# A routed feed-forward stage: the second bias once per token instead of once per block, and three moves of order

## The chip, the core and the metric

The kernel runs on one core of a Trainium2 chip. The metric is device time in microseconds for one launch. The core has five engines with instruction streams of their own: TensorE (PE; PEld is its weight load), VectorE (DVE), ScalarE (ACT), GpSimd (POOL) and SyncE (SP). They meet through semaphores. SyncE and GpSimd also issue the DMAs, each on a queue of its own; 16 DMA engines serve both queues.

## What is computed

```python
def reference(x, src, dst, edge_type_8, ...):
    x = x + gnn(layernorm(x), src, dst, edge_type_8, ...)      # graph layer, 8 relations, gate
    x = x + ffn(layernorm(x)[None], Wr, br, W1, b1, W2, b2, gamma, beta)[0]
    return x

def ffn(tgt, Wr, br, W1, b1, W2, b2, gamma, beta):             # tgt: 1250 tokens x 1024
    logits = einsum('bsd,ed->bse', tgt, Wr) + br               # 8 experts
    top_v, top_i = top_k(logits, 2)
    router_w = sum(one_hot(top_i) * softmax(top_v)[..., None], axis=-2)
    h = relu(einsum('bsd,efd->bsef', tgt, W1) + b1)            # 512 hidden
    o = einsum('bsef,edf->bsed', h, W2) + b2                   # b2: one row of 1024 for each expert
    return layer_norm(tgt + einsum('bsed,bse->bsd', o, router_w)) * gamma + beta
```

The change lies in `ffn` alone. A token's output is its row plus, for each of its two experts, the share times (hidden times W2, plus that expert's b2).

## The kernel before

The tokens are ten tiles of 128 rows (the last has 98). After the graph layer and its gate (until 1718 us of the profiled execution) each tile is normalized, and its rows are stored three times: to the output, to `t_rows` (what the experts read) and to `sum_rows` (where the experts' parts are added). TensorE makes the router's logits from a high and a low half of each row; for this a tile gives two columns per expert, and `turn_logits` (L1312) turns them to rows and adds the halves with a small matmul pair. VectorE then picks the top two (L1449 on).

The routing stage (1718 to 1737 us) sorts the 2500 (token, expert) pairs into at most 27 blocks of 128 rows, so that a block has one expert. VectorE builds one-hot tables, TensorE multiplies them into a list of tokens (L1567) and a list of shares (L1573), and VectorE writes `token_at` and `row_at`, the addresses of a block's token rows and sum rows.

The expert stage (from 1737 us) goes through the blocks b = 0 to 26. All products take the operands apart into a high and a low part and make three matmuls for one. TensorE's order in block b (L2177 on) is: `first(b)`, 24 matmuls with W1; `token_tile(b + 1)`, 8 transposes of the next block's token rows; `second(b - 1, 0)`, the left half of the product with W2 of the block before; `hidden_transposed(b)`; `second(b - 1, 1)`, the right half. Each half of `second` begins with one matmul of 72 rows that puts the block's b2 into PSUM (L2136: a one-hot column `bias_at` against b2, of which the high and low parts lie at rows 0 and 32).

ScalarE splits the token rows (`token_hi`), makes the hidden layer and writes the block's output, times the share, to one of two slots of `o_s` (`output`, L1869). VectorE makes the low parts.

GpSimd's queue (L1820 on) has in block b: for b under 10, add beta to ten tiles of the output, one in each; `gather_tokens(b + 3)`, the rows of a block three further on; `scatter(b - 1)` (L1787), the add of a block's 128 output rows to `sum_rows`. A scatter waits until ScalarE has written both halves of the output and until the scatter before has landed. `output(b, 0)` waits until scatter b - 2 has landed, since it writes the same slot. SyncE's queue loads the experts' split weights, two halves of 4 MB for each expert, into a ring of four halves; a load waits until the half before has landed and until TensorE is done with the expert two before.

The end: when the first 22 scatters have landed, GpSimd loads all ten tiles of `sum_rows` (L1792) into `acc`, where ScalarE and VectorE normalize them beside the last blocks (`bulk_stats`, `scale`); the finished tiles are added to the output by indirect DMAs that leave out tokens with a row in the last five blocks (`store_bulk`, L1816). Tokens of the last five blocks (22 to 26) are done at the very end: `gather_sums` (L1796) fetches their sums into `acc` tiles 0 to 3 and one token slot, so the stores of tiles 0 to 3 have to land first; then come statistics and scaling, and `place` (L1808) adds them to the output.

## Time and profile before

| | |
|---|---|
| time, median of 3 runs | 2137.72 us (2135.85 to 2140.92) |
| the profiled execution | 2136.19 us, of which its span is 2134.5 us |
| busy: PE, DVE, ACT, POOL | 2010.5, 1252.6, 985.2, 921.5 us (94%, 59%, 46%, 43% of the span) |
| gate stage ends, routing ends, experts begin on PE | 1718, 1737, 1743 us |
| PE's last matmul ends | 2100 us |

A row of the timeline has the start in us from the span's start, the time the group took, the engine, the line, the operation with output and inputs, the count, and in brackets how long the engine stood idle before it and what ended that. A matmul's time runs until its result is out; the next one starts earlier, so what one costs is the distance between starts. A DMA row on POOL or SP is the issue; the transfer lands later.

### The profile page before, as it was taken

The page shows a single profiled execution, that of the slowest core. Times are in us where ns is not written, and L with a number is a line of the kernel's source. Part 1 is how long each engine was busy: PE and PEld are TensorE (multiplying, and loading weights), DVE is VectorE, ACT ScalarE, POOL GpSimd, SP SyncE. Part 2 cuts the span into 40 slices and gives each one's busy share as a digit, 9 for nine tenths or more (in the row PEclk, how much of TensorE's full clock was granted, in tenths as well). Part 3 has the DMA queues.
Part 4 walks back from the last instruction along what each step waited for, and adds up shares of the span by engine and source line. Part 5 has one row for each costly group of instructions (what it writes and reads, how often), then busy time and mean ns, then how long its engine had stood idle before and what let it go on. Part 6 is the DMA issues. An engine that isn't in the chain of part 4 may idle for free. (4 is left out here: it accounts for less than half of the span.)

```text
span 2134.5 us, 27951 instructions
## 1 busy us (share of the span) xinstructions
PE 2010.5 (94%) x9385; PEld 1599.8 (75%) x9385; DVE 1252.6 (59%) x2315; ACT 985.2 (46%) x1541; POOL 921.5 (43%) x813
## 2 busy tenths in 40 slices
PE   7999999999999999999989999899889859999993
PEld 6777777777777777787868777677478748788882
DVE  7589878852222222216999988888978842222245
ACT  3211122222222222217999999999844313333355
POOL 0000036555556656406777878778600012221226
PEclk9999999999999999999999999999999959999997
DMA  5322277787778777768788889989867579998757
GB/s 187 104 81 78 76 246 248 252 267 256 252 248 263 248 253 251 251 203 296 260 307 300 321 287 335 338 301 319 296 188 236 172 300 326 332 285 294 223 135 156
DMA packets 156360, 521.55 MB, mean 244 GB/s; under 512 B 31362, under 2 KB 31746, under 8 KB 154186
## 3 DMA queue, kind: packets, MB, share of 16 engines
q1 hardware_dynamic: 83706, 308.63, 41.5%
q0 software_dynamic: 72528, 211.35, 32.2%
q8 instruction: 67, 1.10, 0.2%
q14 instruction: 59, 0.48, 0.1%
HBM read 385.49 MB, written 156.25 MB: 254 GB/s over the span
## 5 line engine op out<-in xcount | busy, mean ns | idle before, releaser
L221 PE MATMUL psum<-w_hi,xnT_hi 128*128 128x512 f32 (+1 forms) x1592 | 420.2, 398 | 9.9 <-issue 5.0
L221 PE MATMUL psum<-w_lo,xnT_hi 128*128 128x512 f32 (+1 forms) x1592 | 419.5, 394 | 0.0
L221 PE MATMUL psum<-w_hi,xnT_lo 128*128 128x512 f32 (+1 forms) x1592 | 413.0, 394 | 0.0
L590 ACT ACTIVATE work<-psum 128x512 f32<-128x512 f32 (+1 forms) x150 | 89.6, 598 | 674.7 <-PE psum L221 674.7
L924 POOL DMA_INDIRECT sorted_rows<-acc x313 | 337.4, 1078 | 116.4 <-issue 84.8
L221 PEld LDWEIGHTS psum<-w_hi,xnT_hi 128*128 128x128 f32 (+1 forms) x1592 | 292.3, 186 | 80.5 <-issue 9.1
L221 PEld LDWEIGHTS psum<-w_lo,xnT_hi 128*128 128x128 f32 (+1 forms) x1592 | 295.4, 186 | 74.4
L221 PEld LDWEIGHTS psum<-w_hi,xnT_lo 128*128 128x128 f32 (+1 forms) x1592 | 294.6, 185 | 71.9
L1040 POOL DMA_INDIRECT w_hi<-y_rows,sort_row x168 | 226.7, 1350 | 63.8 <-issue 40.7
L1040 POOL DMA_INDIRECT w_lo<-y_rows,sort_row x164 | 215.8, 1316 | 62.7 <-issue 42.1
L1125 DVE SCALAR_TENSOR_TENSOR w_hi<-w_hi,sort_recip,y_hi 128x1024 fp32r<-128x1024 f32 x168 | 213.7, 1283 | 35.7 <-ACT y_hi L1086 30.7
L1165 PE MATMUL psum<-y_hi,hot 128*128 128x512 f32 x664 | 213.5, 403 | 12.9 <-ACT y_hi L1086 12.4
L1125 DVE SCALAR_TENSOR_TENSOR w_lo<-w_lo,sort_recip,y_hi 128x1024 fp32r<-128x1024 f32 x164 | 207.9, 1283 | 29.8 <-ACT y_hi L1086 25.5
L212 DVE TENSOR_TENSOR w_lo<-w_raw,w_hi 128x1024 fp32r<-128x1024 f32 x86 | 104.9, 1225 | 189.0 <-ACT w_hi L206 188.4
L892 DVE TENSOR_TENSOR acc<-acc 128x1024 fp32r<-128x1024 f32 x64 | 78.5, 1226 | 220.5 <-ACT acc L599 220.5
L1086 ACT ACTIVATE y_hi<-w_hi,sort_recip 128x1024 fp32r<-128x1024 f32 x168 | 192.1, 1144 | 12.9 <-DMA w_hi<-y_rows,sort_row 3.7
L1086 ACT ACTIVATE y_hi<-w_lo,sort_recip 128x1024 fp32r<-128x1024 f32 x164 | 187.6, 1144 | 10.4 <-DVE w_lo L1125 1.7
L1165 PEld LDWEIGHTS psum<-y_hi,hot 128*128 128x128 f32 x664 | 125.1, 192 | 51.2 <-ACT y_hi L1086 17.5
L921 POOL TENSOR_TENSOR gate_word<-gate_word 1x1 f32<-1x1 f32 x40 | 12.0, 300 | 345.0 <-DVE acc L860 204.6
L1787 POOL DMA_INDIRECT sum_rows<-o_s,row_at x25 | 39.6, 1585 | 241.2 <-DMA sum_rows<-o_s,row_at 130.2
L1051 ACT ACTIVATE apart<-lanes,sort_local 128x128 f16<-128x128 f32 x332 | 127.2, 386 | 6.0 <-DVE lanes L1100 6.0
L1172 PE MATMUL psum<-w_hi,hot 128*128 128x512 f32 x336 | 111.2, 413 | 7.5 <-DVE w_hi L1125 7.1
(378 smaller groups left out, 2645.0 us busy)
## 6 DMA issues: line engine op xcount, KB each, us to landing
split_experts<-acc SPq DMA_DIRECT2D x128, 512.0 KB
ring<-split_experts SPq DMA_DIRECT2D x16, 4096.0 KB, 15.7
w_raw<-in_wchunks SPq DMA_DIRECT2D x86, 512.0 KB, 5.1
y_rows<-work SPq DMA_DIRECT2D x144, 256.0 KB, 2.8
acc<-in_wchunks SPq DMA_DIRECT2D x64, 512.0 KB, 6.0
work<-local_rows SPq DMA_DIRECT2D x26, 384.0 KB, 4.5
acc<-in_bias SPq DMA_DIRECT2D x10, 512.0 KB, 5.6
sorted_rows<-acc POOLq DMA_INDIRECT x313, 4.6
```

The lines of the kernel that those rows point to most:

```text
L212: v.tensor_tensor(w_lo[:, s, q * PIECE:(q + 1) * PIECE], raw_piece(c, q), w_hi[:, s, q * PIECE:(q + 1) * PIECE].bitcast(F32), ALU.subtract)\
L221: i = pe.matmul(to[:rm, :], x_[:, k, m * P:m * P + rm], w_[:, s, k * HALF:(k + 1) * HALF], start=(n == 0), stop=(n == 3 * KD - 1))
L590: act.activation(stage_y[:rows(m), t % 4, :], bank[t % 4][:rows(m), :], ACT.Copy)\
L892: v.tensor_tensor(x_lo[:, p % 2, :], x_raw[:, p % 2, :], x_hi[:, p % 2, :].bitcast(F32), ALU.subtract).then_inc(x_lo_done, 1)
L924: pool.indirect_dma_start(sorted_dram, IndirectOffsetOnAxis(ap=e_dest[:, c:c + 1], axis=0), e_rec[:, c, :], None, bounds_check=BLOCKS * P ...
L1040: pool.indirect_dma_start(slot_of(b).bitcast(F32), None, y_dram, IndirectOffsetOnAxis(ap=sort_row[:, COLUMN[j]:COLUMN[j] + 1], axis=0), bo ...
L1051: act.activation(apart[:, k, :], lanes[:, :], ACT.Square, bias=sort_local[:, at:at + 1], scale=-1.0)\
L1086: act.activation(y_hi[:, j % 2, :], slot_of(b).bitcast(F32), ACT.Copy, scale=sort_recip[:, COLUMN[j]:COLUMN[j] + 1]).then_inc(hi_done, 1)
L1125: v.scalar_tensor_tensor(out=slot_of(b), in0=slot_of(b).bitcast(F32), scalar=sort_recip[:, COLUMN[j]:COLUMN[j] + 1], in1=y_hi[:, j % 2, :] ...
L1165: o = pe.matmul(bank[two + q], hot[:, h, k, :], y_hi[:, j % 2, q * HALF:(q + 1) * HALF], start=first, stop=False)
L1172: o = pe.matmul(bank[two + q], hot[:, h, k, :], slot_of(b)[:, q * HALF:(q + 1) * HALF], start=False, stop=last)
L1787: pool.indirect_dma_start(sum_dram, IndirectOffsetOnAxis(ap=row_at[:, b:b + 1], axis=0), o_s[:, b % 2, :], None, compute_op=ALU.add).then_ ...
```

## The change

1. **The second bias.** The bias matmuls of `second` go. Routing now makes a table `route_of` (for each token its shares of the eight experts, three times: twice the share and once what rounding takes from it). In blocks 2 to 11 TensorE turns one tile of the table (`turn_route`), ScalarE copies it, TensorE multiplies it with b2 (`biases`, two matmuls), and VectorE copies the result to `acc`. In blocks 12 to 21 GpSimd adds one tile of it to `sum_rows` (`add_bias`).
2. **Logits.** The small sum over the halves is taken for tiles 0 to 7 ahead of the last tile's transposes, and for tiles 8 and 9 together at the end.
3. **Routing.** VectorE writes `token_at` and `row_at` ahead of the last one-hot table; it also makes `route_of`.
4. **The end.** The sums of blocks 24, 25 and 26 are gathered into the three token slots, so two tiles of `acc` are needed again and not four. Tiles 0 and 1 are scaled ahead of a tile's statistics in block 25 and stored ahead of the last scatter; gamma is loaded by GpSimd in block 21.

```diff
-B2_AT = (0, 32)
+B2_AT = (0, 32, 64)
...
+                    if s == TILES:
+                        turn_logits(TILES - 2, range(TILES - 2))
...
-                        if m == TILES - 1:
-                            turn_logits(TILES - 1, range(TILES - 1))
...
-                turn_logits(TILES, [TILES - 1])
+                turn_logits(TILES, [TILES - 2, TILES - 1])
...
             def sum_slot(f):
 
-                return t_s[:, 0, :] if f == LAST else acc[:, f - FIRST_LATE, :]
+                if f < LAST - 2:
+                    return acc[:, f - FIRST_LATE, :]
+                return w_raw[:, 0, :] if f == LAST else t_s[:, f - LAST + 2, :]
...
+                def add_bias(m):
+
+                    pool.wait_ge(bias_out, m + 1)
+                    pool.dma_start(sum_dram[m * P:m * P + rows(m), :], acc[:rows(m), m, :], accum_op=ALU.add)\
+                        .then_inc(bias_added, 16)
...
+                    if b == LAST - 1:
+                        for m in range(2):
+                            store_bulk(m)
+                    m = b - TILES - FIRST_BIAS
+                    if 0 <= m < TILES:
+                        pool.wait_ge(o_added, 16 * (b - 1))
+                        add_bias(m)
+                        if m == TILES - 1:
+                            pool.dma_start(gamma_bc[:, :], gamma[0:1, :].to_broadcast([P, D])).then_inc(const_in, 16)
+                        pool.wait_ge(bias_added, 16 * (m + 1))
                     if 1 <= b < LAST:
                         scatter(b - 1)
-                    if b == LAST - 1:
-                        for m in range(4):
-                            store_bulk(m)
                 pool.wait_ge(o_added, 16 * (LAST - 1))
-                pool.wait_ge(bulk_stored[0], 64)
                 pool.wait_ge(t_free, BLOCKS_T)
-                for f in range(FIRST_LATE, BLOCKS_T):
+                for f in range(LAST - 2, BLOCKS_T):
                     gather_sums(f)
-                for m in range(4, TILES):
+                pool.wait_ge(bulk_stored[0], 32)
+                for f in range(FIRST_LATE, LAST - 2):
+                    gather_sums(f)
+                for m in range(2, TILES):
                     store_bulk(m)
...
                     if b == LAST - 1:
+                        for m in (0, 1):
+                            scale(m)
                         bulk_stats(2, 5)
                     if b + 1 < BLOCKS_T:
                         token_hi(b + 1)
+                    m = b - FIRST_BIAS
+                    if 0 <= m < TILES:
+                        act.wait_ge(turned_then_biased, 2 * m + 1)
+                        act.activation(routeT[:, m % 2, :], bank[6][:B2_K, 0:P], ACT.Copy).then_inc(route_copied, 1)
...
                     hidden_lo(b)
+                    m = b - FIRST_BIAS
+                    if 0 <= m < TILES:
+                        v.wait_ge(turned_then_biased, 2 * m + 2)
+                        v.tensor_copy(acc[:rows(m), m, :], psum[:rows(m), 6:8, :].rearrange("p b n -> p (b n)")).then_inc(bias_out, 1)
...
-                    pe.matmul(bank[q], bias_at[:B2_K, b:b + 1].to_broadcast([B2_K, P]), b2_s[:, q * HALF:(q + 1) * HALF],
-                              start=True, stop=False)
...
+                def biases(m):
+
+                    pe.wait_ge(route_copied, m + 1)
+                    if m == 0:
+                        pe.wait_ge(b2_ready, 2)
+                    for q in range(2):
+                        i = pe.matmul(bank[6 + q][:rows(m), :], routeT[:, m % 2, 0:rows(m)], b2_s[:, q * HALF:(q + 1) * HALF],
+                                      start=True, stop=True)
+                    i.then_inc(turned_then_biased, 1)
```

GpSimd's queue from block 21 to the bulk load, before; `e_ostored` counts landed scatters, `e_oread` ScalarE's output halves, `e_tfree` read token slots, `f_bin0` to `f_bin2` the bulk rows:

```order
L1493 DMA t_s<-t_rows,token_at 128x1024 [waits e_tfree]
L1787 DMA sum_rows<-o_s,row_at 1408x1024 [waits e_ostored,e_oread]
L1493 DMA w_raw<-t_rows,token_at 128x1024 [waits e_tfree]
L1792 DMA acc<-sum_rows 128x1024 [waits e_ostored]
L1792 DMA acc<-sum_rows 128x1024 x8
L1792 DMA acc<-sum_rows 98x1024
L1787 DMA sum_rows<-o_s,row_at 1408x1024 [waits e_oread,f_bin2,e_ostored,f_bin1,f_bin0]
```

The same queue now, from block 20 on; `e_bout` counts VectorE's copies of the bias product and `e_badd` landed bias adds:

```order
L1494 DMA w_raw<-t_rows,token_at 128x1024 [waits e_tfree]
L1808 DMA sum_rows<-acc 128x1024 [waits e_bout,e_ostored]
L1802 DMA sum_rows<-o_s,row_at 1408x1024 [waits e_ostored,e_oread,e_badd]
L1494 DMA t_s<-t_rows,token_at 128x1024 [waits e_tfree]
L1808 DMA sum_rows<-acc 98x1024 [waits e_bout,e_ostored]
L1862 DMA gamma_bc<-in_gamma 128x1024
L1802 DMA sum_rows<-o_s,row_at 1408x1024 [waits e_ostored,e_oread,e_badd]
L1494 DMA t_s<-t_rows,token_at 128x1024 [waits e_tfree]
L1802 DMA sum_rows<-o_s,row_at 1408x1024 [waits e_ostored,e_oread]
L1494 DMA w_raw<-t_rows,token_at 128x1024 [waits e_tfree]
L1813 DMA acc<-sum_rows 128x1024 [waits e_ostored]
```

A bias add stands between each gather of token rows and the scatter of blocks 12 to 21, and both waits are on landings.

TensorE at the end of the gate stage, both kernels in one piece (L1368 makes logits, L1317 is the small sum, L157 a transpose):

```order
+L1317 MATMUL psum<-pair_sum,lgT 128x8 x8
 L157 MATMUL psum<-ident,acc 128x98 x8
 L1368 MATMUL psum<-opT_hi,wr_pair 16x128 x8
 L1368 MATMUL psum<-opT_lo,wr_pair 16x128 x8
-L1317 MATMUL psum<-pair_sum,lgT 128x8 x9
 L1368 MATMUL psum<-opT_hi,wr_pair 16x98 x8
 L1368 MATMUL psum<-opT_lo,wr_pair 16x98 x8
+L1317 MATMUL psum<-pair_sum,lgT 128x8
 L1317 MATMUL psum<-pair_sum,lgT 98x8
 L1377 MATMUL psum<-w_raw,r_tri 128x160
```

Eight of the nine sums moved up ahead of the last tile's transposes, and one moved down behind its logits.

GpSimd's end, before (from the last two scatters on):

```order
L1787 DMA sum_rows<-o_s,row_at 1408x1024 [waits e_ostored,e_oread] x2
L1816 DMA out<-acc,bulk_at 1250x1024 [waits f_scaled,f_x1b]
L1816 DMA out<-acc,bulk_at 1250x1024 [waits f_scaled] x3
L1796 DMA acc<-sum_rows,row_at 128x1024 [waits e_tfree,f_bst0,e_ostored]
L1796 DMA acc<-sum_rows,row_at 128x1024 x3
L1796 DMA t_s<-sum_rows,row_at 128x1024
L1816 DMA out<-acc,bulk_at 1250x1024 [waits f_scaled] x6
L1808 DMA out<-acc,final_at 1250x1024 [waits f_y,f_late]
```

And now, from the last scatter but one (`f_bst0` counts the first landed stores):

```order
L1802 DMA sum_rows<-o_s,row_at 1408x1024 [waits e_ostored,e_oread]
L1837 DMA out<-acc,bulk_at 1250x1024 [waits f_scaled,f_x1b]
L1837 DMA out<-acc,bulk_at 1250x1024 [waits f_scaled]
L1802 DMA sum_rows<-o_s,row_at 1408x1024 [waits e_ostored,e_oread]
L1817 DMA t_s<-sum_rows,row_at 128x1024 [waits e_tfree,e_ostored]
L1817 DMA t_s<-sum_rows,row_at 128x1024
L1817 DMA w_raw<-sum_rows,row_at 128x1024
L1817 DMA acc<-sum_rows,row_at 128x1024 [waits f_bst0]
L1817 DMA acc<-sum_rows,row_at 128x1024
L1837 DMA out<-acc,bulk_at 1250x1024 [waits f_scaled] x8
L1829 DMA out<-acc,final_at 1250x1024 [waits f_y,f_late]
```

Two stores moved ahead of the last scatter, two behind the gathers, and three gathers no longer wait for a store.

## Rows read from the trace of the kernel before

**Rows 1.** Busy us by stretch: PE, PEld, DVE, ACT, POOL; clock, DMA share, GB/s

```profile
1770.50:1901.40 130.90, 127.58 (x621) 105.97 (x620) 26.71 (x40) 41.20 (x100) 34.48 (x28) 1.00 0.97 309
1901.40:2003.10 101.70, 101.70 (x497) 84.90 (x496) 21.38 (x32) 33.20 (x80) 20.90 (x16) 1.00 0.88 300
```

**Rows 2.** Timeline of PE, one block of the expert stage

```profile
1901.43 3.79 PE L2126 MATMUL psum<-ring,tT_hi 128*128 x16
...
1906.88 1.04 PE L157 MATMUL psum<-ident,t_s 128*128 128x128 f32 x8
1907.67 0.48 PE L2136 MATMUL psum<-b_s,bias_at 72*128 72x512 f32 x1
1907.99 2.00 PE L2148 MATMUL psum<-ring,hT_hi 128*128 x8
...
1914.14 3.79 PE L2126 MATMUL psum<-ring,tT_hi 128*128 x16
```

**Rows 3.** The bias matmuls: count, ns min/median/max, first and last start, form

```profile
L2136 PE MATMUL psum<-b_s,bias_at x54: 399/481/792, 1764.1 to 2096.6; 72*128 72x512 f32 x54
```

**Rows 4.** Timeline of POOL: scatters (L1787) and the start of the bulk load

```profile
1896.54 1.57 POOL L1787 DMA_INDIRECT sum_rows<-o_s,row_at  x1 [14.67 <-DMA sum_rows<-o_s,row_at]
...
1911.94 1.57 POOL L1787 DMA_INDIRECT sum_rows<-o_s,row_at  x1 [12.49 <-ACT o_s L1869]
...
1919.57 1.57 POOL L1787 DMA_INDIRECT sum_rows<-o_s,row_at  x1 [4.71 <-issue]
...
1949.59 1.57 POOL L1787 DMA_INDIRECT sum_rows<-o_s,row_at  x1 [13.17 <-DMA sum_rows<-o_s,row_at]
...
1956.64 1.57 POOL L1787 DMA_INDIRECT sum_rows<-o_s,row_at  x1 [4.14 <-DMA sum_rows<-o_s,row_at]
...
2043.40 1.57 POOL L1787 DMA_INDIRECT sum_rows<-o_s,row_at  x1 [9.79 <-ACT o_s L1869]
...
2049.78 5.39 POOL L1792 DMA_DIRECT2D acc<-sum_rows  x10 [3.46 <-DMA sum_rows<-o_s,row_at]
...
2083.22 1.56 POOL L1787 DMA_INDIRECT sum_rows<-o_s,row_at  x1 [5.75 <-ACT acc L1919]
```

**Rows 5.** Line L1787, the 25 scatters: from issue to landing

```profile
DMA to landing us min/median/max: 6.1/11.3/17.0
```

**Rows 6.** Line L1301, the ten adds of the gate bias: from issue to landing

```profile
DMA to landing us min/median/max: 4.7/5.2/7.7
```

**Rows 7.** Timeline of SP's queue: weight loads (L1502), issues

```profile
1895.82 0.33 SPq L1502 DMA_DIRECT2D ring<-split_experts  x1
...
1914.49 76.60 SPq L1502 DMA_DIRECT2D ring<-split_experts  x5
```

**Rows 8.** Waits, 1764 to 2134 us: who for whom, total us, times, longest

```profile
POOL sum_rows L1787 <- DMA sum_rows<-o_s,row_at: 130.2, 14, 14.7
...
PE psum L157 <- DMA t_s<-t_rows,token_at: 3.5, 3, 3.0
```

**Rows 9.** Timeline of PE: end of the gate stage, start of the expert stage

```profile
1702.81 1.57 PE L157 MATMUL psum<-ident,acc 98*128 98x98 f32 x8 [5.97 <-DVE acc L1428]
...
1706.44 4.00 PE L1317 MATMUL psum<-pair_sum,lgT 16*128 16x8 f32 x18 [0.36 <-ACT lgT L1280]
...
1742.74 1.97 PE L157 MATMUL psum<-ident,t_s 128*128 128x128 f32 x8 [7.46 <-DMA t_s<-t_rows,token_at]
```

**Rows 10.** Timeline of ACT: first statistics of bulk rows and of late sums

```profile
2058.72 1.03 ACT L1897 ACTIVATE psum<-acc 128x1024 f32<-128x1024 f32 x1 [2.79 <-DMA acc<-sum_rows]
...
2107.45 1.06 ACT L1897 ACTIVATE t_s<-acc 128x1024 f32<-128x1024 f32 x1 [10.17 <-issue]
```

**Rows 11.** Timeline of POOL at the end: first gather of sums, two stores

```profile
2101.00 1.00 POOL L1796 DMA_INDIRECT acc<-sum_rows,row_at  x1 [7.50 <-issue]
...
2107.33 1.60 POOL L1816 DMA_INDIRECT out<-acc,bulk_at  x1 [0.30 <-issue]
2109.24 1.57 POOL L1816 DMA_INDIRECT out<-acc,bulk_at  x1 [0.31 <-issue]
```

More of the change, by code:

```diff
@@ L1316, in turn_logits @@
                     for m in tiles:
-                        i = pe.matmul(bank[2 if m < TILES - 1 else 3][:rows(m), m * E:(m + 1) * E], lgT[:, m * P:m * P + rows(m)], pair_sum[:, :],
+                        i = pe.matmul(bank[2 if m < TILES - 2 else 3][:rows(m), m * E:(m + 1) * E], lgT[:, m * P:m * P + rows(m)], pair_sum[:, :],
                                       start=True, stop=True)
@@ L1440, in _ @@
                 three_d, lg = [P, TILES, E], router[:, :, :]
-                for at, need, rm in ((slice(0, TILES - 1), 1, P), (slice(TILES - 1, TILES), 2, rows(TILES - 1))):
+                for at, need, rm in ((slice(0, TILES - 2), 1, P), (slice(TILES - 2, TILES - 1), 2, P),
+                                     (slice(TILES - 1, TILES), 2, rows(TILES - 1))):
                     v.wait_ge(lg_rows, need)
@@ L1623, in _ @@
                                         part_w[:, h, :].bitcast(F32).unsqueeze(2).to_broadcast([P, COLS, LISTS]), ALU.mult)
+                for k in range(2):
+                    i = v.tensor_tensor(shares[:, k, :, :], chosen[:, :, k * TILES:(k + 1) * TILES].rearrange("p e t -> p t e"),
+                                        weight_of[:, k, :].unsqueeze(2).to_broadcast([P, TILES, E]), ALU.mult)
+                link(i)
+                v.wait_ge(lists_done, 1)
+                v.tensor_scalar(empty[:, :], bank[2][:, 0:TILES_T], 0.0, None, ALU.is_equal)
+                link(v.tensor_scalar(tokens[:, :], bank[2][:, 0:TILES_T], -1.0, None, ALU.add))
+                v.scalar_tensor_tensor(out=token_at[:, :], in0=empty[:, :], scalar=float(Y_PAD), in1=tokens[:, :],
+                                       op0=ALU.mult, op1=ALU.add).then_inc(tabled, 1)
+                v.scalar_tensor_tensor(out=row_at[:, :], in0=empty[:, :], scalar=spare_row[:, 0:1], in1=tokens[:, :],
+                                       op0=ALU.mult, op1=ALU.add)
+                v.memset(route_of, 0.0)
+                link(v.tensor_tensor(shares[:, 0, :, :], shares[:, 0, :, :], shares[:, 1, :, :], ALU.add))
+                v.tensor_copy(route_of[:, :, B2_AT[0]:B2_AT[0] + E], shares[:, 0, :, :])
+                link(v.tensor_copy(shares_hi[:, :, :], shares[:, 0, :, :]))
+                v.tensor_copy(route_of[:, :, B2_AT[1]:B2_AT[1] + E], shares[:, 0, :, :])
+                v.tensor_tensor(route_of[:, :, B2_AT[2]:B2_AT[2] + E], shares[:, 0, :, :], shares_hi[:, :, :].bitcast(F32), ALU.subtract)
                 v.tensor_tensor(not_last[:, 0, :], place[:, 0:TILES], place[:, TILES:COLS], ALU.is_lt)
@@ L1846, in _ @@
                     place(f)
[L1847 removed]
+                pool.wait_ge(bulk_stored[1], 16 * (TILES - 2 + LATE))
             @block.scalar
@@ L1950, in _ @@
                         output(b - 1, 1)
-                    if b == LAST - 1:
-                        for m in (0, 1):
-                            scale(m)
-                for m in range(4, 8):
+                for m in range(4, 7):
                     scale(m)
-                act.wait_ge(t_free, BLOCKS_T)
-                for n, f in ((5, LAST - 4), (6, LAST - 3), (7, LAST - 2)):
+                late_stats(5, LAST - 2)
+                for m in range(7, 10):
+                    scale(m)
+                for n, f in ((6, LAST - 4), (7, LAST - 3)):
                     late_stats(n, f)
-                for m in (8, 9):
-                    scale(m)
                 for f in range(FIRST_LATE, LAST):
@@ L2147, in second, with turn_route @@
                             n += 1
-                            i = pe.matmul(bank[q], x_[:, k, :], w_, start=False, stop=(n == 3 * KF))
+                            i = pe.matmul(bank[q], x_[:, k, :], w_, start=(n == 1), stop=(n == 3 * KF))
                     i.then_inc(s2_done if q else o_first, 1)
+                def turn_route(m):
+                    if m == 0:
+                        pe.wait_ge(late_ready, 3)
+                    else:
+                        pe.wait_ge(bias_out, m)
+                    transpose(pe, bank[6][:B2_K, 0:P], route_of[:, m, :]).then_inc(turned_then_biased, 1)
+                def biases(m):
+                    pe.wait_ge(route_copied, m + 1)
+                    if m == 0:
+                        pe.wait_ge(b2_ready, 2)
[3 more added lines that the diff above has]
+                    i.then_inc(turned_then_biased, 1)
                 def spread_tokens():
```

62 lines of the change are left out of this document (29 added, 33 removed).

## The prediction

> **What bounds the kernel now.** I read the stretches by engine first [rows 1], then one block of the expert stage on TensorE [rows 2], then the chain of waits on GpSimd's queue [rows 4] and the list of waits [rows 8]. In blocks 12 to 19 TensorE is busy for all of 101.70 us and the 16 DMA engines for 0.88 of it [rows 1]. A block takes 1914.14 - 1901.43 = 12.71 us [rows 2], so TensorE is the bound. A second resource stands right beside it. GpSimd issues one scatter-add of a finished block to the sum rows at a time, and each waits until the one before has landed: 14 such waits, 130.2 us [rows 8]. I call the time from one such issue to the next, where only the landing decides, a step. It is 7.63 and 7.05 us where no weight load is under way, on average 7.3 (1911.94 to 1919.57 and 1949.59 to 1956.64 [rows 4]), and 15.4 us where a 4 MB load shares the engines (1896.54 to 1911.94, a load issued at 1895.82 [rows 4, 7]), so one load costs the chain 8.1 us. Five steps with three loads in them (1895.82, 1914.49 and the next some 19 us on [rows 7]) should then take 5 x 7.3 + 3 x 8.1 = 60.8 us; it was 1956.64 - 1896.54 = 60.1 [rows 4]. The chain needs about 12 us per block and has 12.71: it is nearly full. It already reaches TensorE, since the gather of token rows three blocks ahead stands behind each scatter on the same queue; TensorE stood 3.5 us for such rows [rows 8], in the stretch in which beta is also added to the output over that queue and the DMA share is 0.97 [rows 1].
>
> **The change part by part.** All sums are made against the profiled execution: span 2134.5 us, 2136.19 with the 1.7 us around it, 1.5 below the median of 2137.72.
>
> Logits. 4.00 us of small matmuls (the sum of two halves for nine tiles) lie between the logits of tile 8 and those of tile 9, while TensorE sat idle for 5.97 us just before, waiting for the last tile [rows 9]. The change puts eight of the nine tiles into that idle time; their inputs are there, since the last of them is tile 7. Two matmuls of tile 8 come back at the end (a half of 0.5 us) and one more small VectorE addition of 0.2. Nothing else ends that wait: **-3.3 us**.
>
> Token addresses. VectorE writes them ahead of a few small operations, about 1 us sooner, but also does some 2 us more for the new table of shares, and the second small sum is later. The first token rows land at 1742.74, after 7.46 us of waiting for a transfer that runs beside two weight loads [rows 9]; the added VectorE work ends ahead of that. I take 0, with 1 us to either side.
>
> TensorE in the expert stage. Each of the 54 bias matmuls [rows 3] holds the next matmul up by 1907.99 - 1907.67 = 0.32 us [rows 2], so 0.64 per block goes. In blocks 2 to 11 one transpose (about 0.15, from 8 in 0.79 [rows 2]) and two matmuls of the same 72-row form (0.64) come back: +0.15 per block. So by block 12 the work stands at -3.3 - 0.6 + 1.5 = -2.4 us. From block 12 on a block could take 12.07 us. ScalarE's copy of the shares and VectorE's copy of the bias product are hidden: a block leaves ScalarE two thirds and VectorE four fifths of its time [rows 1], and the next transpose that waits for VectorE's copy stands behind 5.4 us of first-layer matmuls. If that cover were gone, it would cost about 1 us in each of ten blocks.
>
> **GpSimd's queue, blocks 12 to 21.** Here the change adds a wait, and it decides. Ahead of each scatter now stands a bias add of 128 rows of 4 KB to the same sum rows: it waits until the last scatter has landed, and the next scatter waits until it has landed. Behind that stand, on the same queue, the scatter and then the token gather for a block two and a half blocks away, for which TensorE waits. No row shows such an add without other traffic. The nearest are the scatter, of the same size and into the same rows, at 6.1 us to landing at least [rows 5], and the add of the gate bias, same form and size but into SBUF, at 4.7, 5.2 at the median [rows 6]. A step is 1.2 us longer than the landing (7.3 against 6.1), so a bias add is a step of 5.9 to 7.3; I take 6.9, near the scatter. A pair takes 7.3 + 6.9 = 14.2 us, over 12.07 even without a load. The loads of the second half are issued from 1914.49 on over 76.60 us, five of them [rows 7], and wait for TensorE's progress, so they stay inside the chain however long it gets: four whole ones and some 0.6 of another. Ten pairs take 142 + 4.6 x 8.1 = 179 us. They begin when scatter 10 has landed, 1919.57 - 2.4 = 1917 [rows 4], so scatter 21 goes out at 2096 instead of 2043.40. Its slack is soon used up: a gather goes out two and a half blocks of 12.07 us ahead of its use and needs some 10 to land, so TensorE can run some 20 us (an estimate) ahead of the queue, and the first two or three pairs take that.
>
> End. The bulk load of the sum rows begins 6.4 us after scatter 21 (2043.40 to 2049.78 [rows 4]): 2102.4. From there to the last scatter it is 2083.22 - 2049.78 = 33.4 us now. It gets longer: ScalarE's program has two tile statistics, which wait 8.9 us for the first group (2049.78 to 2058.72 [rows 4, 10]), ahead of the token copy for block 25. TensorE now stands already and can do nothing in that time, and two scalings are also moved ahead of the copy for block 26. I take 38, between 33 and 42. After the last scatter it is 51.3 us now: 17.8 to the first gather of sums, of which 7.50 wait for four stores of bulk rows [rows 11], and 33.5 from there on. With three of the sums in free slots the first gather needs only the scatter's landing, 7.3; against that, eight stores instead of six lie ahead of the placements (2109.24 - 2107.33 = 1.9 each [rows 11]). ScalarE's statistics, which start 6.4 us after the first gather [rows 10, 11], run beside them, so of these 3.8 us I add 1.2: 7.3 + 33.5 + 1.2 = 42 us, so -9.3.
>
> **Sum:** 2102.4 + 38 + 42 = 2182.4 us of span, and 1.7 around it: 2184 us, 48 above the profiled execution.
>
> The Trainium skill's page "DMA: Bandwidth & Descriptors" (section "Anatomy of one DMA — SWDGE (gpsimd) path") speaks for a much cheaper add: about 2.0 us plus the bytes at 436 GB/s, an estimate of 3.2 us for 512 KB. The scatter of the same bytes took at least 6.1 [rows 5], so the trace does not agree; by that figure the pair would fit and the first rival would hold.
>
> **The rivals.** (1) *The add is short and hides; faster.* A block has 12.07 us, the scatter takes 7.3 and the loads 3.7 of it; with 20 us of lead to spend over ten blocks, a step of the add under about 3.1 us would leave TensorE the bound. Then -2.4, -6.4 for blocks 12 to 21, -3.2 for the five after, -9.3 at the end and +4.6 before the last scatter: 2136.2 - 16.7 = 2119.5 us. For it speaks that the DMA engines are idle for 0.12 of the time [rows 1]; against it that the shortest landing of a like add is 4.7 us, before any load [rows 6]. (2) *The engines' total time and not the waits is the limit.* The stretch with beta keeps them busy 0.97 x 130.90 / 10 = 12.7 us per block, the one without 0.88 x 101.70 / 8 = 11.2 [rows 1]. With bias adds in place of beta's, blocks 12 to 21 then stay at about 12.7 us as now, and the rest holds: 2136.2 - 2.4 - 3.2 - 9.3 + 4.6 = 2126 us. Against it: the waits stand in the program one behind the other. (3) *A load hits the add and the scatter alike.* Each 4 MB load then costs 16.2 instead of 8.1: +37, 2221 us. Against it: the load has a fixed number of pieces to put between the others, and the five-step check held with 8.1. (4) *Cheap adds, loads that fall into the waits between transfers:* steps of 6.4, half the price of a load: 137 + 18 = 155, so 2160 us.
>
> **How the numbers follow.** The main case has 0.68 (2165 to 2203), case 4 0.12, case 3 0.09, case 1 0.07, case 2 0.04. The range of 8 in 10 takes in the main case, most of case 4 and the lower part of case 3: 2150 to 2210. Faster by over 0.2% (about what a measurement tells from no change here): case 1 and most of case 2, 0.10. Within it, where cases 2 and 4 meet: 0.03. Slower: 0.87.
>
> **What would show it.** Right: in the waits of the expert stage, GpSimd's scatter and the new add each wait for the other's landing some ten times, a pair 14 us apart without a load and over 20 with one; TensorE stands for token rows in blocks 14 to 22, over 40 us together; the first gather of sums comes 7 to 8 us after the last scatter; the top two begin 3.3 us sooner. Wrong: pairs 12 us apart and TensorE busy throughout blocks 12 to 21 (case 1 or 2); pairs of 20 us and more after the last load (a step of the add far over 7).

## The result, and the profile after

| | before | after |
|---|---|---|
| time, median of 4 runs each | 2139.32 us (2135.85 to 2144.04) | 2177.17 us (2174.82 to 2181.03) |
| ratio, 95% interval | 1 | 1.0165 (1.0142 to 1.0188) |
| span of the profiled execution | 2134.5 us | 2178.9 us |

The change makes the kernel slower by 37.9 us. What runs ahead of the changed code takes some us more or less from run to run: the matmul that counts the chosen pairs (L1377) begins between 1708 and 1723 us in the profiles of this study. So I compare traces from that matmul on. From there to the end it is 417.8 us before (2134.5 - 1716.68) and 460.2 after (2178.9 - 1718.68): +42.4; ahead of it 3.6 are gained.

GpSimd's queue after; L1808 is the new bias add, L1802 the scatter, L1813 the bulk load, L1817 the late sums. Columns as in [rows 4].

```profile
1920.32 0.98 POOL L1808 DMA_DIRECT2D sum_rows<-acc  x1 [3.81 <-DMA sum_rows<-o_s,row_at]
1935.91 1.60 POOL L1802 DMA_INDIRECT sum_rows<-o_s,row_at  x1 [14.62 <-DMA sum_rows<-acc]
...
1953.44 0.95 POOL L1808 DMA_DIRECT2D sum_rows<-acc  x1 [14.54 <-DMA sum_rows<-o_s,row_at]
1959.18 1.60 POOL L1802 DMA_INDIRECT sum_rows<-o_s,row_at  x1 [4.80 <-DMA sum_rows<-acc]
...
2050.79 1.60 POOL L1802 DMA_INDIRECT sum_rows<-o_s,row_at  x1 [4.69 <-DMA sum_rows<-acc]
...
2057.24 0.95 POOL L1808 DMA_DIRECT2D sum_rows<-acc  x1 [3.48 <-DMA sum_rows<-o_s,row_at]
2063.01 1.60 POOL L1802 DMA_INDIRECT sum_rows<-o_s,row_at  x1 [4.82 <-DMA sum_rows<-acc]
...
2094.64 1.57 POOL L1802 DMA_INDIRECT sum_rows<-o_s,row_at  x1 [4.03 <-ACT o_s L1899]
...
2101.15 5.38 POOL L1813 DMA_DIRECT2D acc<-sum_rows  x10 [3.23 <-DMA sum_rows<-o_s,row_at]
...
2135.92 1.53 POOL L1802 DMA_INDIRECT sum_rows<-o_s,row_at  x1 [4.28 <-ACT o_s L1899]
2142.46 1.78 POOL L1817 DMA_INDIRECT t_s<-sum_rows,row_at  x1 [5.01 <-DMA sum_rows<-o_s,row_at]
```

Every add waits for a scatter and every scatter for an add. A pair takes 2063.01 - 2050.79 = 12.2 us where no weight load is under way. A step beside a load takes 15.6 (1920.32 to 1935.91) or 17.5 (1935.91 to 1953.44). The ten pairs take 2094.64 - 1920.32 = 174.3 us. TensorE leaves them 10 x 12.25 = 122.5.

Landing of the add (L1808) and of the scatter (L1802), after:

```profile
DMA to landing us min/median/max: 5.1/5.4/15.9
...
DMA to landing us min/median/max: 6.0/6.5/18.0
```

Waits from 1755 to 2180 us, after (total, times, longest), to be held against [rows 8]:

```profile
ACT o_s L1899 <- DMA sum_rows<-o_s,row_at: 129.1, 14, 25.2
...
POOL sum_rows L1802 <- DMA sum_rows<-acc: 77.2, 10, 15.2
POOL sum_rows L1808 <- DMA sum_rows<-o_s,row_at: 56.9, 10, 14.5
...
PE psum L157 <- DMA t_s<-t_rows,token_at: 33.5, 5, 16.3
```

The wait for each other is there in both directions, ten times each. It reaches ScalarE, which may not overwrite `o_s` (129.1 us; the row of before stands below), and TensorE, whose token rows stand behind it on the queue: 33.5 us where it was 3.5 [rows 8].

```profile
ACT o_s L1869 <- DMA sum_rows<-o_s,row_at: 4.6, 2, 2.4
```

TensorE after, four block starts and the three long stalls:

```profile
1772.29 3.79 PE L2163 MATMUL psum<-ring,tT_hi 128*128 x16
...
1785.14 3.79 PE L2163 MATMUL psum<-ring,tT_hi 128*128 x16
...
1963.75 3.79 PE L2163 MATMUL psum<-ring,tT_hi 128*128 x16
...
1976.00 3.79 PE L2163 MATMUL psum<-ring,tT_hi 128*128 x16
```

```profile
1954.35 1.97 PE L157 MATMUL psum<-ident,t_s 128*128 128x128 f32 x8 [5.30 <-DMA t_s<-t_rows,token_at]
...
1997.86 1.97 PE L157 MATMUL psum<-ident,t_s 128*128 128x128 f32 x8 [16.25 <-DMA t_s<-t_rows,token_at]
...
2046.11 1.97 PE L157 MATMUL psum<-ident,t_s 128*128 128x128 f32 x8 [8.34 <-DMA t_s<-t_rows,token_at]
```

A block with a bias tile takes 1785.14 - 1772.29 = 12.85 us (12.84 in most others), one without any bias 1976.00 - 1963.75 = 12.25; before it was 12.71 [rows 2]. Behind each long stall eight transposes take 1.97 us and not 1.04 [rows 2]: TensorE begins again at the lower of its two clock levels (1.2 GHz and not 2.4). The stretch around the first of them, columns as in [rows 1], has a granted clock of 0.55:

```profile
1953.00:1960.00 7.00, 5.56 (x18) 4.47 (x19) 2.58 (x4) 4.10 (x10) 1.77 (x2) 0.55 0.49 78
```

### The profile page after: what moved, and what is told of

Its sections match the earlier page's. It is cut to its first block and busy times, and to the rows that moved or that the text cites. A ratio compares the mean times of both kernels' runs of the same rounds, so it can differ in the third digit from the quotient of the medians.

```text
span 2178.9 us, 27955 instructions
## 1 busy us (share of the span) xinstructions
PE 2021.9 (93%) x9361; PEld 1605.8 (74%) x9361; DVE 1265.6 (58%) x2333; ACT 987.8 (45%) x1551; POOL 934.6 (43%) x824
## 5 line engine op out<-in xcount | busy, mean ns | idle before, releaser
L1086 ACT ACTIVATE y_hi<-w_hi,sort_recip 128x1024 fp32r<-128x1024 f32 x168 | 192.0, 1143 | 15.4 <-DMA w_hi<-y_rows,sort_row 5.4
L2015 DVE TENSOR_TENSOR hT_lo<-w_raw,hT_hi 128x512 fp32r<-128x512 f32 x26 | 18.0, 693 | 202.2 <-ACT hT_hi L1915 202.1
L1802 POOL DMA_INDIRECT sum_rows<-o_s,row_at x25 | 40.3, 1612 | 219.0 <-ACT o_s L1899 90.5
## 6 DMA issues: line engine op xcount, KB each, us to landing
ring<-split_experts SPq DMA_DIRECT2D x16, 4096.0 KB, 15.9
```

Of the source, the lines that this page charges most:

```text
L1086: act.activation(y_hi[:, j % 2, :], slot_of(b).bitcast(F32), ACT.Copy, scale=sort_recip[:, COLUMN[j]:COLUMN[j] + 1]).then_inc(hi_done, 1)
```

## The experiments

Theory A: the time goes into two accumulating DMAs that wait for each other on one queue, and a weight load lengthens each wait that it falls on. Rival B: the added traffic costs it. Rival C: the bias work of blocks 2 to 11 or the new order at the end costs it. The table gives each run's time beside the kernel before on the same chip, and the stretch from the counting matmul to the end of its profile (417.8 before, 460.2 after). A stretch belongs to one execution: that of x_add_16rows was the fastest of nine (2138.02 us), that of x_add_out the slowest of ten (2143.30), that of x_moves_fine 6.9 us over its median (2149.75). In x_logits the code behind the counting matmul is that of the kernel before, and the stretch is 4.2 us longer, so a difference of that size tells nothing.

| run | time | before there | ratio, 95% | stretch |
|---|---|---|---|---|
| x_no_add | 2133.31 | 2142.29 | 0.9939 (0.9914 to 0.9963) | 411.7 |
| x_add_out | 2136.65 | 2142.29 | 0.9977 (0.9963 to 0.9990) | 418.0 |
| x_moves | 2132.10 | 2142.29 | 0.9948 (0.9932 to 0.9965) | 414.3 |
| x_bulk_add | 2150.27 | 2142.29 | 1.0038 (1.0018 to 1.0059) | 435.3 |
| x_small_loads | 2132.71 | 2142.84 | 0.9954 (0.9939 to 0.9969) | 411.2 |
| x_add_pairs | 2161.90 | 2142.84 | 1.0092 (1.0076 to 1.0108) | 446.3 |
| x_add_16rows | 2148.02 | 2142.84 | 1.0028 (1.0011 to 1.0044) | 428.0 |
| x_logits | 2137.40 | 2142.84 | 0.9972 (0.9957 to 0.9986) | 422.0 |
| x_fine_loads | 2166.00 | 2142.41 | 1.0105 (1.0060 to 1.0150) | 442.4 |
| x_moves_fine | 2142.90 | 2142.41 | 0.9998 (0.9981 to 1.0016) | 428.2 |
| x_beta_late | 2136.94 | 2142.41 | 0.9963 (0.9945 to 0.9981) | 416.8 |
| x_moves_mixed | 2127.48 | 2144.33 | 0.9924 (0.9906 to 0.9941) | 407.3 |

**Without the adds.** In `for b`, `add_bias(m)` and its two waits go.

```diff
-                        pool.wait_ge(o_added, 16 * (b - 1))
-                        add_bias(m)
...
-                        pool.wait_ge(bias_added, 16 * (m + 1))
```

> The changed kernel without the ten adds of the bias tiles to the sum rows in blocks 12 to 21 and without their waits; the tiles are still made in blocks 2 to 11, so the second bias is missing from the output. Theory A (the two accumulations that wait for each other on GpSimd's queue cost the time): TensorE is the bound again in blocks 12 to 21, at 12.2 us per block, and the time is the kernel before less what the other parts give: 2139.3 - 3.6 (logits) - 6.4 (bias matmuls, 27 x 0.46 less 10 x 0.6) - 8.3 (end) + 1.4 (bulk load to last scatter) = 2122 us, between 2117 and 2128. Rival B (the 10 x 512 KB of added traffic cost it): also about 2122, since the traffic goes too. Rival C (the loss lies in the bias work of blocks 2 to 11 or in the new order at the end): 2155 or more.

C falls: the loss is gone with the adds. But 9 us are gained and not 17. Three of the nine single runs took 2122.5 to 2123.9 us, as A has it, the other six 2129.0 to 2138.3; the profile is of one of the six (2129.02). In the profile 411.7 us stand where 417.8 - 6.4 - 8.3 + 1.4 = 404.5 were expected. TensorE waits for token rows around block 9, where beta shares the queue:

```profile
1858.82 3.79 PE L2160 MATMUL psum<-ring,tT_hi 128*128 x16
1867.70 1.97 PE L157 MATMUL psum<-ident,t_s 128*128 128x128 f32 x8 [3.27 <-DMA t_s<-t_rows,token_at]
1877.85 3.79 PE L2160 MATMUL psum<-ring,tT_hi 128*128 x16
```

This block takes 1877.85 - 1858.82 = 19.03 us and not 12.84. Before, a block at the same place waits almost as long, 3.05 us (first row below), and takes 15.98. Nearly all of the difference is the clock: 0.71 here from the transposes on (last row), 1.00 before (second row).

```profile
1868.67 1.09 PE L157 MATMUL psum<-ident,t_s 128*128 128x128 f32 x8 [3.05 <-DMA t_s<-t_rows,token_at]
...
1868.00:1876.00 8.00, 7.33 (x38) 6.22 (x39) 1.29 (x2) 2.81 (x7) 3.70 (x3) 1.00 0.84 152
```

```profile
1867.00:1878.00 11.00, 10.30 (x40) 8.68 (x41) 1.29 (x2) 3.07 (x8) 3.69 (x3) 0.71 0.87 153
```

So 2.9 of the missing 7.2 us come from this block, 0.2 of them from a longer wait and the others from a lower clock behind it. Of the rest 1.5 lie at the end (2126.9 - 2082.39 = 44.5 us from the last scatter on, where 43.0 were counted on) and 1.2 in a block that waits for ScalarE's output (13.45 us and not 12.25, from 2001.52); I have not placed what is left.

**The same adds, but meeting no scatter.** The target of the ten adds is the output, and both waits go. In their place the first add waits until the adds of beta to the output have landed, and the bulk load until all ten bias adds have.

```diff
-                    pool.dma_start(sum_dram[m * P:m * P + rows(m), :], acc[:rows(m), m, :], accum_op=ALU.add)\
+                    pool.dma_start(out[m * P:m * P + rows(m), :], acc[:rows(m), m, :], accum_op=ALU.add)\
```

> The changed kernel with the ten adds of 512 KB from the same place of the queue, in the same form, but into the rows of the output and not of the sum rows: they meet no scatter, so neither waits for the other (one wait for all ten ahead of the bulk load). The second bias so reaches the output past the normalization. The traffic is that of the changed kernel. Theory A (waits): 2122 us as without the adds, and up to 10 more since an add stands ahead of a scatter on the same queue: 2122 to 2133; GpSimd's scatter and bias add no longer wait for each other, TensorE waits under 10 us for token rows. Rival B (traffic): nearly as slow as the changed kernel, 2160 or more.

B falls: with the full traffic the time is 3.3 us above the run without the adds, and 40 below the changed kernel. A has the mechanism; its range ended at 2133, 3.7 us short. The waits (total, times, longest) no longer name the add:

```profile
POOL sum_rows L1802 <- ACT o_s L1900: 145.1, 14, 15.0
...
POOL sum_rows L1802 <- DMA sum_rows<-o_s,row_at: 77.4, 9, 14.2
...
PE psum L157 <- DMA t_s<-t_rows,token_at: 9.8, 3, 4.8
```

**The other moves alone**, built from both kernels: bias by matmul as before, all else as after.

> The kernel before with the other moves alone (logits, order of the routing, three late sums in the token slots, two tiles scaled and stored sooner, gamma by GpSimd in block 21); the second bias by one matmul for each half in each block, as before. Theory A: 2139.3 - 3.6 (logits) - 8.3 (end) + 1.4 = 2129 us, between 2125 and 2133. Rival: if the end's gain came only from the sums being late anyway in the changed kernel, the end stays at 51 us and the time at 2136.

A holds. The end's gain is real: the last scatter goes out at 2088.07 and the span ends at 2131.2, so 43.1 us against 51.3 before. And the median is that of the run without adds (2132.1 and 2133.3): moving the bias off the matmuls would bring nothing at the median even if the adds were free. In three of nine runs it brought some 9 us (2122.5 to 2123.9); what decides between these runs and the others is not shown.

**The price of the loads.** From the twelfth half on a load fetches 64 of its 8192 columns.

```diff
+                        if n < SMALL_FROM:
+                            load_half(sp, n, row + n % 2 * P)
+                        else:
+                            sp.dma_start(ring[:, n // 2 % 2, n % 2, 0, 0:64].bitcast(F32),
+                                         we_dram[bass.ds(row + n % 2 * P, P), 0:64]).then_inc(half_in[n % RING], 16)
```

> The changed kernel with the last five weight loads (those issued beside the chain of bias adds and scatters) cut from 32 KB to 256 B per row, so that the last experts work with old weights; all adds and waits stay. In the changed kernel's trace a step of the chain is about 6 us without a load and 16 with one, five of twenty steps with one. Theory A (a load costs the chain 10 us each time, and the add itself some 6): ten pairs take 10 x 12.3 = 123 us and not 174, just TensorE's own 12.25 per block, and the time falls to that of the kernel without the adds, 2133 us, or up to 8 above: 2127 to 2141. Rival (the added wait itself is too long, loads or not): the time stays above 2157, less than 20 us gained.

A holds, and to the number. All waits and adds are there, and the chain keeps pace with TensorE: ten of TensorE's blocks without idle time (columns as in [rows 1]), then GpSimd's queue, first add, one pair and scatter 21.

```profile
1914.60:2037.00 122.40, 122.40 (x601) 102.30 (x600) 26.85 (x40) 41.25 (x100) 35.29 (x30) 1.00 0.65 116
```

```profile
1919.88 0.98 POOL L1813 DMA_DIRECT2D sum_rows<-acc  x1 [4.30 <-DMA sum_rows<-o_s,row_at]
...
1975.76 1.61 POOL L1807 DMA_INDIRECT sum_rows<-o_s,row_at  x1 [4.64 <-DMA sum_rows<-acc]
...
1987.88 1.59 POOL L1807 DMA_INDIRECT sum_rows<-o_s,row_at  x1 [4.67 <-DMA sum_rows<-acc]
...
2044.61 1.57 POOL L1807 DMA_INDIRECT sum_rows<-o_s,row_at  x1 [3.91 <-DMA sum_rows<-o_s,row_at]
```

Ten pairs in 2044.61 - 1919.88 = 124.7 us. In the changed kernel 174.3, with five loads: (174.3 - 124.7) / 5 = 9.9 us a load. So the mutual wait alone fits: a pair of 12.1 us here (1975.76 to 1987.88) against a block of 12.25. It is the loads that carry the chain past TensorE.

**The price of the bytes.** Sixteen rows and not 128 in each add, all waits kept.

```diff
-                    pool.dma_start(sum_dram[m * P:m * P + rows(m), :], acc[:rows(m), m, :], accum_op=ALU.add)\
+                    pool.dma_start(sum_dram[m * P:m * P + 16, :], acc[:16, m, :], accum_op=ALU.add)\
```

> The changed kernel with each bias add cut from 128 rows to 16, one row for each DMA engine; all waits stay, and the other rows lack the second bias. It tells the fixed price of the wait from that of the bytes. Theory A (most of an add's 5.4 us to landing is bytes and pieces of the load between them): step of the add under 4 us without a load and under 8 with one, chain under TensorE's 12.25 per block, 2131 to 2142. Rival (most is a fixed price of issue and landing): step over 5 us, and 2155 or more.

Both miss the time (2148.02, from 2138.02 to 2152.92; the profile is of the fastest run). The add's landing (first row) and four rows of GpSimd's queue:

```profile
DMA to landing us min/median/max: 2.7/2.7/12.2
```

```profile
1909.46 0.89 POOL L1808 DMA_DIRECT2D sum_rows<-acc  x1 [3.55 <-DMA sum_rows<-o_s,row_at]
1922.09 1.61 POOL L1802 DMA_INDIRECT sum_rows<-o_s,row_at  x1 [11.73 <-DMA sum_rows<-acc]
...
2020.70 0.88 POOL L1808 DMA_DIRECT2D sum_rows<-acc  x1 [3.35 <-DMA sum_rows<-o_s,row_at]
2023.68 1.62 POOL L1802 DMA_INDIRECT sum_rows<-o_s,row_at  x1 [2.11 <-DMA sum_rows<-acc]
```

Without a load the step is 3.0 us, as A says: of 5.4 us to landing 2.7 stay with 64 KB, and 2.7 are the other 448 KB. What A had wrong is the load. It holds up a 64 KB add too, in a step of 12.6 us the first time, and else it falls mostly on the scatter that comes next. The ten pairs take 2049.71 - 1909.46 = 140.3 us; without loads they would take 10 x 9.4 (6.4 for the scatter, 3.0 for the add), so a load still costs some 9 us (an estimate) beside adds of an eighth of the size.

**Two adds in one wait.** `add_bias(m - 1)` and `add_bias(m)` in every second block, and one wait for both.

> The changed kernel with the bias adds issued two at a time in every second block (rows of different tiles do not meet), with one wait for both: five waits of scatters for adds and not ten. Theory A (what is paid is the wait for a landing, not the bytes): two adds in flight land in 1 to 3 us more than one, so two blocks of the chain take 2 x 6.4 + 7 to 9 + one load's 10 = 30 to 32 us and not 34.9, 15 to 25 us in all: 2152 to 2162. Rival (an add costs by its bytes, one after the other): no gain, 2170 to 2180.

A holds, at its upper edge: 15.3 us less than the changed kernel. Two adds in flight make a step of 9.2 us without a load:

```profile
1970.90 1.88 POOL L1808 DMA_DIRECT2D sum_rows<-acc  x2 [3.26 <-DMA sum_rows<-o_s,row_at]
1980.13 1.60 POOL L1802 DMA_INDIRECT sum_rows<-o_s,row_at  x1 [7.35 <-DMA sum_rows<-acc]
```

**Bias rows kept off the chain.** Tiles are written plainly to memory of their own, the bulk load adds into the tiles that still hold the bias, and late sums are added onto gathered bias rows.

```diff
-                    pool.dma_start(sum_dram[m * P:m * P + rows(m), :], acc[:rows(m), m, :], accum_op=ALU.add)\
+                    pool.dma_start(bias_dram[m * P:m * P + rows(m), :], acc[:rows(m), m, :])\
...
-                    pool.dma_start(bulk_slot(m), sum_dram[m * P:m * P + rows(m), :]).then_inc(...)
+                    pool.dma_start(bulk_slot(m), sum_dram[m * P:m * P + rows(m), :], accum_op=ALU.add).then_inc(...)
```

> The changed kernel with the bias rows kept off the scatters' chain: in blocks 12 to 21 each tile is written plainly to rows of its own in memory, with no wait; the bulk load of the sum rows adds into the tiles in SBUF, which still hold the bias; the late sums are added onto bias rows that are gathered ahead of the last scatter's landing. Theory A: no wait between a scatter and the bias, so 2122 us as without the adds, and 0 to 6 more for ten plain writes, an adding bulk load and five small gathers: 2122 to 2128, under the moves alone by 1 to 7. Rival B (traffic): ten writes of 512 KB and ten adding loads cost 10 us or more: 2132 or above.

Theory A failed, mostly at the end of the kernel and not on the chain:

```profile
2050.60 9.09 POOL L1814 DMA_DIRECT2D acc<-sum_rows  x10 [3.42 <-DMA sum_rows<-o_s,row_at]
2080.50 2.13 POOL L1803 DMA_INDIRECT sum_rows<-o_s,row_at  x1 [20.82 <-DMA acc<-sum_rows]
...
2094.93 1.53 POOL L1803 DMA_INDIRECT sum_rows<-o_s,row_at  x1 [1.13 <-DMA sum_rows<-o_s,row_at]
```

From the bulk load to the next scatter 29.9 us pass, and 2066.29 - 2047.63 = 18.7 with plain loads in the run without adds:

```profile
2047.63 5.37 POOL L1813 DMA_DIRECT2D acc<-sum_rows  x10 [3.49 <-DMA sum_rows<-o_s,row_at]
2066.29 1.68 POOL L1802 DMA_INDIRECT sum_rows<-o_s,row_at  x1 [13.29 <-DMA acc<-sum_rows]
```

From the last scatter to the end it is 2148.1 - 2094.93 = 53.2 us, against 44.5 in the run without adds. One block also waits 3.65 us for token rows and takes 19.16. So rival B has the time (2132 or above). The adding loads still cost less than the waits that they save, since the time is 27 us below that of the changed kernel; they cost more than the whole change gains without the adds, and the version is 8 us slower than the kernel before.

**The logits alone.** The diff is that of the change.

> The kernel before with the move of the logits' small sums alone. Theory A: the top two begin 3.3 to 3.6 us sooner and all that follows moves with them: ratio 0.9984, 2139 of 2142. Rival: around block 10, while beta is added over the same queue, TensorE waits for token rows anyway, so what is gained ahead is lost there: ratio 1.000 within 0.001.

By the times the rival is out: the ratio's interval ends at 0.9986. Its centre, -6 us, is more than the move can give (3.6 in the trace); the interval reaches down to 3. The one profile does not bear this out: there TensorE stands 1.90 and 3.09 us for token rows in blocks 8 and 9 (0.27 and 3.05 before), and the stretch behind the counting matmul is 4.2 us longer. So what is gained ahead can be lost there, as the rival says, and in this execution it was.

**Shorter pieces.** Each row of a load is 32 KB in one piece; here eight DMAs of 4 KB a row, in the changed kernel and in the moves alone.

```diff
+            for j in range(LOAD_PIECES):
+                at = slice(j * (2 * CW // LOAD_PIECES), (j + 1) * (2 * CW // LOAD_PIECES))
+                sp.dma_start(ring[:, n // 2 % 2, n % 2, :, :].rearrange("p k n -> p (k n)")[:, at].bitcast(F32),
+                             we_dram[bass.ds(row, P), at]).then_inc(half_in[n % RING], 16)
```

> The changed kernel, all of it, but each 4 MB weight load is issued as eight DMAs of 512 KB whose pieces are 4 KB long and not 32 KB. Theory A: a load costs a step of the chain 10 us because its long pieces stand between the short ones (4 KB) of the add or scatter; with pieces of one size the engines are shared evenly, a step beside a load takes 2 to 4 us more and not 10, ten pairs 140 to 150 us and not 174, and the time is 2133 to 2145. Rival (a load costs by its bytes, which are the same): 2172 to 2182.

> The kernel before with the other moves (bias by matmul) and the same loads in 4 KB pieces. Theory A: the 5 to 7 us in which TensorE waits for token rows around blocks 8 to 10, beside loads and beta, shrink too: 2124 to 2131. Rival (the engines' total time is the limit in that stretch, 0.97 busy): 2132 as the moves alone, or a few us above since eight DMAs have more to begin and end.

All four forecasts miss the times (2166.00 and 2142.90). What A says of the stalls is half right. Blocks 2 to 11 run without a stall in both, at 12.84 and 12.71 us, and in the changed kernel the ten pairs take 2075.11 - 1913.51 = 161.6 us: less than 174.3, not the 140 to 150 of A. But loads follow one another, and in pieces each takes longer beside short DMAs: the halves beside beta are issued 23 to 27 us apart in the moves (from 1783.55 to 1884.52), and 18 to 20 in the kernel before. From block 12 on TensorE waits for weights (L1782 is where SyncE reports a landed half). The moves with 4 KB pieces (total, times, longest):

```profile
PE psum L2138 <- SPq L1782: 15.3, 3, 12.5
```

**Beta later**, in blocks 12 to 21: `if 12 <= b < 12 + TILES` in place of `if b < TILES`.

> The kernel before with the other moves, and beta added in blocks 12 to 21 and not in 0 to 9. In blocks 0 to 11 the DMA engines are 0.97 busy, in 12 to 21 0.75, and TensorE waits 5 to 7 us for token rows around blocks 8 to 10. Theory A (beta's adds cause that wait, and behind block 12 there is room for them since nothing waits for them): 2126 to 2129. Rival (there they lengthen the scatters' steps, the chain reaches TensorE as the bias adds did): 2132 or more.

The rival holds. TensorE waits no more in blocks 8 to 10, and instead in three blocks from 14 on, by 0.63, 3.30 and 2.10 us.

**Pieces mixed**: 4 KB for the seven loads beside beta, 32 KB for the others, on the moves alone.

```diff
+            return 8 if RING <= n < 11 else 1
```

> The kernel before with the other moves, and 4 KB pieces for the seven weight loads that run beside beta (the fifth to the eleventh half) alone; the first four and the last five keep 32 KB pieces. With 4 KB pieces throughout, TensorE no longer waited for token rows in blocks 8 to 10, but from block 12 on it waited 15 us for the weights, whose loads follow one another and take longer each. Theory A: with the pieces mixed, the first gain stays and the loss goes: the moves alone less 5 to 7 us, 2125 to 2129 at the level of the kernel before of 2142. Rival (the weight loads so delayed reach TensorE in the next blocks all the same, or the wait for token rows comes later): 2132 or more.

A holds, and this version is faster than both kernels: 16.9 us under the kernel before. Over the moves alone it gains 4.6 us (2132.10 to 2127.48): on the same chip its six runs all lie below the four of the moves, though the intervals of the two ratios overlap. TensorE has no idle time left in either stretch (columns as in [rows 1]):

```profile
1770.00:1900.00 130.00, 130.00 (x634) 108.38 (x633) 26.73 (x40) 42.37 (x105) 34.51 (x28) 1.00 0.95 277
1900.00:2060.00 160.00, 160.00 (x781) 133.41 (x781) 33.45 (x50) 54.19 (x130) 38.15 (x35) 1.00 0.84 274
```

## Why the prediction was right, step by step

The forecast was 2184 us, the time is 2177.17. That the add and the scatter wait for each other, that loads fall into these waits and that TensorE then stands for token rows is what the runs without waits and with small loads show. One step of the mechanism does not hold: a pair was to take 14.2 us, over TensorE's block "even without a load". It takes 12.2, and with small loads it hides; the loss shows only with the loads. That the total is so near is in part luck, as told below. In the trace it forecast +48 and +38.8 came (42.4 less 3.6). The terms:

| step | forecast | measured |
|---|---|---|
| last tile's transposes to counts | -3.3 | -3.6 (13.87 to 10.27) |
| counts to the first token tile | 0 | -0.4 (26.06 to 25.69) |
| bias matmuls, each block | 0.64 | 0.46 (12.71 to 12.25) |
| tile's transpose and two matmuls, net | +0.15 | +0.13 (12.84) |
| pair without a load | 14.2 us | 12.2 |
| a load | 8.1 us, 4.6 of them | 9.9, five of them |
| ten pairs | 179 us | 174.3 |
| bulk load to last scatter | 38 | 34.8 |
| last scatter to end | 42 | 43.0 |

**Logits and addresses** were right. TensorE from the last sums to the counts, after:

```profile
1702.79 1.95 PE L1317 MATMUL psum<-pair_sum,lgT 16*128 16x8 f32 x16 [0.35 <-ACT lgT L1280]
1708.41 1.57 PE L157 MATMUL psum<-ident,acc 98*128 98x98 f32 x8 [3.66 <-DVE acc L1428]
...
1713.93 0.56 PE L1317 MATMUL psum<-pair_sum,lgT 16*128 16x8 f32 x4 [0.33 <-ACT lgT L1280]
1718.68 0.87 PE L1377 MATMUL psum<-w_raw,r_tri 128*128 128x160 f32 x2 [4.19 <-DVE w_raw L1461]
```

Sixteen small matmuls take 1.95 us out of what was idle time (3.66 remain of 5.97 [rows 9]), and four stand at the end.

**TensorE's blocks.** The distance of 0.32 us behind a bias matmul overstated its price, since the next matmul's own wait is in it. Both prices came out lower, so the net of blocks 2 to 11 stayed. What the prediction left out is that work saved ahead of block 10 need not arrive behind it: TensorE waits around blocks 8 to 10 for token rows that come beside loads and beta, at a price of 6.2 us in the run without adds.

**GpSimd's queue.** The total of the ten pairs is 2.6% off because two sizes were wrong in opposite ways. The add's step was set at 6.9, near the scatter; it is 5.8 (2057.24 to 2063.01), as its landing of 5.4 us is near that of the gate bias [rows 6], the row of the same form. The scatter's step was set at 7.3; it is 6.45 (2050.79 to 2057.24). The price of a load was 9.9 and not 8.1. The two errors have one source: a step beside a load was read as 15.4 and is 15.6 to 17.5, so the step without one, too long by about 1 us, took as much off the difference between them; the rest of the missing 1.8 us lies in the longer steps beside a load. Of the two steps behind that 7.3 the row of one, 7.63, names no landing as its end [rows 4]. A pair of 12 us stood among the signs of being wrong; it came, but TensorE busy throughout, the other half of that sign, did not. Rival 1 (add under 3.1 us) and rival 2 (total time of the engines) fall, the second by the run into the output. Rival 3 falls: a load costs the chain once. Rival 4 was nearer with its pair (7.3 + 6.4 = 13.7 in its sum, 12.2 measured) and wrong with its loads. Rival 1's bound of 3.1 us was too generous: in the run with 16 rows the step was 3.0 and the ten pairs took 140.3 - 122.5 = 17.8 us more than TensorE's blocks, inside the 20 us of lead that the estimate gave it, and TensorE still stood for token rows, 5.23 us the longest time. So the lead is shorter than 20 us.

The Trainium skill's page "DMA: Bandwidth & Descriptors" (section "Anatomy of one DMA — SWDGE (gpsimd) path") puts a DMA that GpSimd issues at about 2.0 us plus its bytes at 436 GB/s. The add of 512 KB landed after 5.4 us and that of 64 KB after 2.7, so the rate is 448 KB in 2.7 us, some 170 GB/s, and the fixed part 2.7 less 0.4 for 64 KB at that rate, 2.3 us (an estimate): for an accumulating DMA the trace agrees with the page on the fixed part, roughly, and not on the rate. Nor would the first rival have held by the page's 3.2 us, as the prediction has it: with the 1.2 us between landing and step it is a step of 4.4, over that rival's 3.1.

**TensorE's stalls** were 33.5 us and not over 40; but a long one also costs the clock. The granted clock was 0.90 between 1910 and 2102 us, and the block with the stall of 16.25 us was 31.67 - 12.25 = 19.4 longer, 3.2 more than the stall.

**The end.** The late sums came 2142.46 - 2135.92 = 6.5 us after the last scatter (7.3 forecast). The 4.6 us that I added between bulk load and last scatter were 1.4 (34.8 against 33.4); TensorE did stand there, 12.44 us once, and why so little of it reached the last scatter I did not follow further.

## What to carry to other kernels

Before a step is moved to a queue, add up what already waits there one behind the other, per block, and compare that with the bound, loads included; here 12 us of 12.7 were taken, and 0.46 us of matmul were exchanged for a wait of 5.8. Price an added DMA by the row of the same form (direct or indirect, adding or plain), and price its meeting with a bulk transfer apart, since here that came once per transfer, at nearly the same price for 64 KB and for 512. Where short transfers on the path share engines with long prefetches, the length of a prefetch's pieces is a knob: cut them only in the stretch where the short ones are late and the prefetch has time.

## What the runs showed of the hardware

- Beside a 4 MB load in 32 KB pieces an add of 64 KB (16 rows) took 12.2 us to landing the one time that it met it from the start (2.7 without), one of 512 KB up to 15.9 (5.4 at the median): nearly the same loss, 10 us.
- With 4 KB pieces blocks 2 to 11 ran without a stall, and steps of the chain beside a load fell from 15.6 to between 7 and 11 us, at the price of loads that took longer: beside beta they were issued 23 to 27 us apart and not 18 to 20.
- Adding loads cost more than plain ones of the same bytes: ten adding loads of up to 512 KB into SBUF took 29.9 us and ten plain ones 18.7, each measured to the next scatter.
- A wait of 3.05 us left TensorE's clock at 1.00, one of 3.27 at the same place was followed by 0.71, and cost 6.2 us and not 3.3. What the stalls around blocks 8 to 10 cost so varies from run to run (3.8 us in the profile before, up to 7.1 in those of the other runs with whole pieces and beta in blocks 0 to 9); that they are gone in the three profiles with shorter pieces there is shown, what sets their length in a single run is not.
